# The B part of the scan's operand built per tile in the first stage, readout ahead of the inputs in two banks, and the weighing by C whole and one unit later

## The reference

```python
x = x + 0.5 * ffn(layernorm(x), w1, b1, w2, b2)
x = x + mamba(layernorm(x), ...)
x = x + 0.5 * ffn(layernorm(x), w1, b1, w2, b2)

# mamba, D_INNER 512, D_STATE 16
xc = silu(causal_conv(xn @ W_in.T))
dt = soft_clamp(softplus(xc @ W_dt.T + b_dt), 0.001, 0.1, 0.5)
Bp, Cp = xc @ W_B.T, xc @ W_C.T
dA = exp(soft_clamp(dt * A, -8, 8, 0.5))
def step(h, ...):
    h = h * dA_t + dt_t * B_t * x_t
    nrm = sqrt(sum(h * h))
    h = where(t % 10 == 0, h * minimum(20 / nrm, 1), h)
    y = sum_n(h * C_t) + D_param * x_t
out = x + scale * (y * silu(gate)) @ W_out.T
```

## Time and profile before

| | |
|---|---|
| median of 3 runs | 1645.36 us (1644.27 to 1646.35) |
| the profiled execution | 1644.98 us, its span 1643.1 us |
| busy, share of the span | PE 89%, DVE 78%, ACT 68%, POOL 60% |
| first stage, a tile | 49.7 us (226.03 to 275.73, the same instruction of two tiles) |
| scan stage, 410 units | 428.3 to 1426.4 us |

### The profile page before, as it was taken

How to read it: one execution, slowest core, us unless ns; L and a number is a source line. 1 busy time by engine, 2 the same in 40 slices (tenths; PEclk the granted TensorE clock), 3 DMA queues, 4 the chain that set the end, 5 groups by cost and what they waited for, 6 DMA issues and landing times. The chain is left out here.

```text
span 1643.1 us, 24197 instructions
## 1 busy us (share of the span) xinstructions
PE 1461.6 (89%) x6460; PEld 986.7 (60%) x6460; DVE 1278.2 (78%) x2555; ACT 1112.3 (68%) x2515; POOL 986.4 (60%) x1350
## 2 busy tenths in 40 slices
PE   6999999999688888888888888888888888999998
PEld 5555555554456566656665656665665665677776
DVE  7657656655578888888887888887888889877885
ACT  4355445557978888888887888887888874243333
POOL 1202222012479898989988889898998999700000
PEclk9999999999789999999999999999999999999999
DMA  7222355125565555656655565555655436465430
GB/s 251 77 79 91 117 146 143 66 92 189 164 182 158 162 152 140 172 149 168 160 154 151 137 174 133 158 161 141 178 153 155 135 98 198 122 208 171 137 116 26
DMA packets 232654, 236.84 MB, mean 144 GB/s; under 512 B 46120, under 2 KB 198376, under 8 KB 232520
## 3 DMA queue, kind: packets, MB, share of 16 engines
q1 hardware_dynamic: 231576, 233.99, 49.7%
q10 hardware_dynamic: 944, 1.31, 0.2%
HBM read 136.84 MB, written 98.68 MB: 143 GB/s over the span
## 5 line engine op out<-in xcount | busy, mean ns | idle before, releaser
L1145 DVE TENSOR_TENSOR_SCAN h<-decay,banks 128x352 f32<-128x352 f32 x820 | 710.5, 882 | 56.8 <-POOL hc L948 1.5
L948 POOL TENSOR_TENSOR hc<-h,bc 128x320 f32<-128x320 f32 x820 | 655.1, 821 | 30.6 <-PE banks L995 28.4
L995 PE MATMUL banks<-hc,w_ident 128*128 128x320 f32 (+1 forms) x1664 | 543.6, 452 | 47.6 <-ACT yc L1084 38.6
L1050 ACT ACTIVATE tb<-dtc,a 128x320 f32<-128x320 f32 (+1 forms) x832 | 416.3, 554 | 4.8 <-DVE x L562 4.8
L995 PEld LDWEIGHTS banks<-hc,w_ident 128*128 128x128 f32 x1664 | 291.8, 196 | 125.5 <-POOL hc L948 39.8
L1072 ACT ACTIVATE decay<-tb 128x640 f32<-128x640 f32 x410 | 296.3, 723 | 0.4
L938 POOL TENSOR_TENSOR rc<-qs,w_mhalf 128x1 f32<-128x1 f32 x410 | 225.9, 551 | 114.9 <-DVE qs L1129 106.0
L983 PE MATMUL banks<-ub 128*128 128x176 f32 x1640 | 283.9, 297 | 10.9 <-DMA ub<-scratch_ub 10.9
L976 PEld LDWEIGHTS banks<-sc_ss,sc_ones 128*128 128x128 f32 x820 | 134.6, 197 | 263.8 <-ACT sc_sq L1061 246.2
L1061 ACT ACTIVATE sc_sq<-h 128x64 f32<-128x64 f32 x410 | 128.1, 313 | 189.1 <-issue 100.0
L983 PEld LDWEIGHTS banks<-ub 128*128 128x128 f32 x1640 | 227.4, 201 | 12.2 <-DMA ub<-scratch_ub 11.2
(11 more groups left out here) (117 smaller groups left out, 1562.1 us busy)
## 6 DMA issues: line engine op xcount, KB each, us to landing
ub<-scratch_ub SPq DMA_DIRECT2D x410, 107.5 KB
bc<-scratch_blk SPq DMA_DIRECT2D x205, 160.0 KB, 3.6
scratch_ub<-turned SPq DMA_DIRECT2D x64, 512.0 KB, 4.1
scratch_ub<-spread SPq DMA_DIRECT2D x64, 176.0 KB, 4.3
scratch_xc<-xc SPq DMA_DIRECT2D x8, 1024.0 KB, 4.8
scratch_sg<-sg SPq DMA_DIRECT2D x8, 1024.0 KB, 5.9
scratch_dt<-dt SPq DMA_DIRECT2D x8, 1024.0 KB, 5.9
scratch_u<-u SPq DMA_DIRECT2D x8, 1024.0 KB, 6.7
```

Source lines behind the costliest of these rows:

```text
L948: pool.tensor_tensor(hc[:, pl % 2, x * kh * B * N:(x + 1) * kh * B * N, j % QB * S:(j % QB + 1) * S] .rearrange("p (c b n) e -> p c b n e" ...
L995: mm = pe.matmul(psY[:, 0:KE * B * wide], w.ident[:], rhs, start=(n == 0), stop=(n == N - 1))
L1050: act.activation(tanh_rows(c, r), dtc[:, c % 2, k * B:(k + 1) * B, 0:blocks_of(c) * S].rearrange("p b (k e) -> p k b e", e=S), ACT.Tanh, s ...
L1145: dve.tensor_tensor_scan(state(m).rearrange("p r e -> p (r e)")[:, half], decay[:, m % DRING, half], psI[m % B][:, half], 0.0, ALU.mult, A ...
```

## The change

- **Weighing**: `weigh(m)` is one operation over all of the state, where it was two halves, and POOL issues `weigh(m-1)` in its turn m.
- **Readout**: in PE's turn m the readout's two matmuls (now for m-1) stand between `total(m+2)` and `inputs(m+2)`; they stood behind `inputs(m+2)`. Quads alternate between two PSUM banks (2 and 5) up to quad 48, and wait for the copy of the quad before the last (`y_before`); `copy_y` comes two units later.
- **B**: it is no longer part of the pieces. PE turns it out of `bcs` for each tile (`turn_b`, a new slot `bt` in the ring), ACT copies it (`copy_bt`), POOL splits and spreads it (`spread_b`, six operations a tile into two buffers), SP stores it (`store_b`, 8 DMAs a tile). The masks are made at tile 0.
- **Pieces**: u alone, one each 10 units, PE's four transposes in four units, ACT's copy in two halves, DVE's part after that; loads and stores at other places of SP's order.
- **Stores**: `dt` and `u` of the last tile go out in eight parts, one a block.

```diff
@@ sync (first stage)
             if i in (6, 7):
                 scan.load_piece(sp, i - 5)
                 scan.store_piece(sp, i - 6)
+            if i >= 2:
+                scan.store_b(sp, i - 2, 0, G)
             sp.wait_ge(xc_ready, 2 * (i + 1))
...
                 scan.load_units(sp)
+                scan.store_b(sp, LAST - 1, 0, G)
@@ gpsimd (first stage)
                 norm2(i + 1)
-            if i in (6, 7):
-                scan.mask_piece(pool, i - 6)
+            if i >= 1:
+                scan.spread_b(pool, i - 1, 0, G)
@@ tensor (first stage)
             project(i, "x", 0)
+            if i >= 1:
+                turn_b(i - 1)
@@ scan stage
+    def spread_b(pool, i, q0, q1):
+        if q0 == 0:
+            pool.wait_ge(pre.ring_read, pre.turn_of["bt", i, 0] + 1)
+            if i >= 1:
+                pool.wait_ge(spread_done, G * i)
+            pool.tensor_copy(bts[:, 0], bt[:]).then_inc(b_split, 1)
+            pool.wait_ge(b_split, 2 * i + 1)
+            pool.tensor_tensor(bts[:, 1], bt[:], bts[:, 0].bitcast(F32), ALU.subtract).then_inc(b_split, 1)
...
+        for q in range(q0, q1):
+            if G * i + q >= 2:
+                pool.wait_ge(b_out[q % 2], 2 * 16 * ((G * i + q) // 2))
+            pool.tensor_tensor(
+                spread[:, q % 2], bts[:, :, q].bitcast(F32).unsqueeze(3).broadcast_to([P, 2, N, W]),
+                mask[:, (i * TT // P + q % 2) % (S // 2)].unsqueeze(1).unsqueeze(1).broadcast_to([P, 2, N, W]),
+                ALU.mult).then_inc(spread_done, 1)
+
+    def store_b(sp, i, q0, q1):
+        for q in range(q0, q1):
+            t = i * TT + q % 2 * P
+            sp.wait_ge(spread_done, G * i + q + 1)
+            for half in range(2):
+                sp.dma_start(
+                    dram["ub"][q // 2, t:t + P].rearrange("t (r h) x -> t r h x", h=2)[:, :, half, E:],
+                    spread[:, q % 2].bitcast(F32).rearrange("p r n e -> p r (n e)")).then_inc(b_out[q % 2], 16)
@@ gpsimd (scan stage)
-            weigh(m, 0)
-            weigh(m, 1)
-            if m - 1 in pieces:
-                mask_piece(pool, pieces[m - 1])
+            if m >= 1:
+                weigh(m - 1)
+            if m in (8, 12, 16, 20):
+                spread_b(pool, TILES - 1, m // 4 - 2, m // 4 - 1)
+        weigh(UNITS - 1)
@@ tensor (scan stage)
         for m in range(UNITS):
             if m + B < UNITS:
                 total(m + B)
-                inputs(m + B)
-            if m in pieces:
-                turn_piece(pe, pieces[m], psT)
...
-            p, part = m // (QB * B) - 1, m % (QB * B)
+            p, part = (m - 1) // (QB * B) - 1, (m - 1) % (QB * B)
             if p >= 0:
                 readout(p, part * each, (part + 1) * each)
+            if m + B < UNITS:
+                inputs(m + B)
+            for c in range(KE):
+                if m - c in pieces:
+                    turn_piece(pe, pieces[m - c], psT, c, c + 1)
```

More of the change, by code:

```diff
@@ L142, in store_dt_u, with store_last, stored @@
         store(sp, "u", u[:], u_out, i)
+    def store_last(sp, k):
+        name, tile, ready, done = ("dt", dt, dt_ready, dt_out) if k < KE else ("u", u, u_ready, u_out)
+        c = k % KE
+        sp.wait_ge(ready, LAST + 1)
+        sp.dma_start(dram[name][:, c * B:(c + 1) * B, steps(LAST)],
+                     tile[:, c, :].rearrange("p (b t) -> p b t", b=B)).then_inc(done, 16)
+    def stored(i):
+        return 16 * (i + 1) if i < LAST else 16 * (LAST + KE)
     def dt_u(dve, i):
@@ L347, in project_bc, with turn_b @@
             mm.then_inc(ring_done, 1)
+        def turn_b(i):
+            out = fill(("bt", i, 0))
+            pe.wait_ge(ring_read, use["bc", i, 0] + 1)
+            for q in range(G):
+                mm = pe.transpose(out[:, q * N:(q + 1) * N], bcs[0:N, q * P:(q + 1) * P], w.ident[0:N, 0:N])
+            mm.then_inc(ring_done, 1)
         pe.wait_ge(consts, 1)
@@ L838, in high_piece, with turn_piece @@
[L838 to L843, removed]
-    def low_piece(dve, k, src):
[L846 to L858, removed]
+    def turn_piece(pe, k, out, c0, c1):
+        if c0 == 0:
+            pe.wait_ge(piece_in, 16 * (k + 1))
+            if k >= 1:
+                pe.wait_ge(ut_lo, k)
+        for c in range(c0, c1):
+            mm = pe.transpose(out[:, c * P:(c + 1) * P], piece[:, c, :], w.ident[:])
+        if c1 == KE:
+            mm.then_inc(ut_done, 1)
@@ L861, in store_piece @@
         t, b = k // B * P, k % B
-        rows = dram["ub"][b, t:t + P].rearrange("t (r h) x -> t r h x", h=2)
         sp.wait_ge(ut_lo, k + 1)
         for r in range(2):
-            sp.dma_start(rows[:, r, :, 0:E], turned[:, :, 0:E].bitcast(F32)).then_inc(ub_out, 16)
-        sp.wait_ge(spread_done, k + 1)
-        for half in range(2):
-            sp.dma_start(rows[:, :, half, E:], spread[:].bitcast(F32).rearrange("p r n e -> p r (n e)")
-                         ).then_inc(ub_out, 16)
+            sp.dma_start(dram["ub"][b, t:t + P, 2 * r:2 * r + 2, 0:E], turned[:].bitcast(F32)).then_inc(ut_out, 16)
@@ L1117, in scalar @@
                 decays(m + AHEAD)
-            if m % (QB * B) == 0 and m >= 2 * QB * B:
+            if m % (QB * B) == 2 and m >= 2 * QB * B:
                 copy_y(m // (QB * B) - 2)
-            if m in pieces:
-                high_piece(act, pieces[m], psT)
-        for p in range((UNITS - 1) // (QB * B) - 1, QUADS):
+            for x in range(2):
+                if m - KE - x in pieces:
+                    high_piece(act, pieces[m - KE - x], psT, x * E // 2, (x + 1) * E // 2)
+        for p in range((UNITS - 3) // (QB * B) - 1, QUADS):
             copy_y(p)
```

154 lines of the change are left out of this document (95 added, 59 removed).

## The result

The changed kernel takes **1717.21 us** (median of 4 runs, 1715.12 to 1720.2) against 1645.86 us (4 runs, 1644.27 to 1647.84): a ratio of **1.0434**, 95% interval 1.0415 to 1.0454. It is slower by 71 us, and the forecast was 1716. The span grew by 70.2 us, to 1713.3.

What follows compares the result with a forecast made beforehand. PE bounds the first stage; in the scan no engine is free of load and stalls add 100 us. First stage +49 and scan +22 give +71 us, 1716 us; range 1664 to 1750, chance of slower 0.90.

Steps and rivals of the forecast that it cites:

- First stage: Tiles ahead of the scan: spreads waiting for stores delay `rstd1` and DVE, with clock loss and transposes; +49 us (33 to 65).
- R: The time in a first-stage tile at which POOL ends `norm2`; `rstd1` was forecast at R + 7.4 to R + 11.0.
- The clock term: PE in the first stage loses clock after each of four pauses, 1.5 us each: 6 us (0 to 10).
- the stalls: First-stage tiles 2 to 5: 3 x 6.5 + 20.3 = 40 us (33 to 47) from `rstd1` behind `spread_b`.
- `turn_b`, 3 us: Four added transposes a tile on busy PE in the first stage, seven times: 3 us, 8 at the high end.
- The loop: Scan: with the readout ahead of the inputs, a two-unit loop from squares to squares takes 4.87 us, 2.44 a unit.
- the rival's point of decision: Scan unit of 2.27 us, the readout adding 0.28 us in place of 0.60, decides whether the first rival holds.
- Scan: Unit of 2.44 against 2.40 us gives +15 us; with pieces, late loads and ends +22 us (0 to +45).
- left over: Scan: disturbances remaining beside the regular unit, pieces 3 us and late `ub` loads 5.2 us, taken as 8 us.
- up to the 100 us: Scan: stalls of 0.27 us per unit, 100 us in all, which the second bank and spread pieces take away.
- the first rival: Scan gains what was removed: units stay at 2.13 us, scan falls 92 us, time 1602; chance 0.08.
- these rivals: First stage doesn't stall: 1670, chance 0.10. PE falls to half clock in the scan: near 1990, chance 0.03.

Runs made afterwards that it cites:

- Kernel 1: The changed kernel with POOL issuing the next turn's `rstd1` ahead of `spread_b` in the first stage instead of behind it: 1675.7 us.
- kernel 5: The changed kernel with `rstd1` ahead of `spread_b` in the first stage and the inputs ahead of the readout in the scan: 1608.6 us.
- Kernel 7: The changed kernel with one of the readout's two matmuls ahead of the inputs and the other behind them: 1652.8 us.
- Kernel 2: The changed kernel with PE issuing the inputs ahead of the readout's two matmuls in the scan, as before the change: 1648.7 us.
- kernel 11: The changed kernel with inputs ahead of the readout and the weighing in two halves, still one unit later: 1651.2 us.
- kernel 3: The kernel before with only the readout and the pieces' transposes placed as in the changed kernel; one bank, halved weighing: 1822.8 us.
- 8: The changed kernel, readout ahead of the inputs, with one PSUM bank for all quads and the copy one unit earlier: 1829.4 us.
- 9: The changed kernel with inputs ahead of the readout and the weighing in two halves in its own unit again: 1802.9 us.

## Why the prediction held, point by point

- **First stage, +49 forecast, +47.0 measured.** The mechanism was read rightly: SP behind `bc` at R + 2.7, `rstd1` at R + 8.6 where the bounds were 7.4 and 11.0, DVE's waits 12.65 and 26.63 us ("some 11", "some 26"), PE's pauses ahead of the gate 5.1 to 10.1 us. The stores are issued in 0.62 us and land in 2.4 (medians up to 425 us), near the low ends: the queues were as empty as supposed. The tiles 2 to 5 are 7.34, 8.17, 21.73 and 7.71 us longer than 49.7, 45 in all. Kernel 1 shows the cause.
- **The clock term, 6 us.** PE was at 0.50 behind the pauses. The gate's 16 matmuls took 8.82, 8.97, 9.22 and 9.83 us in the four tiles, 8.3 us in all over the 7.13 of the earlier trace rows, against my 6. The Trainium skill (TensorE: Matmul & The Clock Gate, section on HAM oscillation) tells of a PE that comes back at half clock from each long wait for data; by it all four pauses pay, and the rows agree. Without these 8.3 the four tiles have some 37 us, where I had 40 for the stalls: two small errors that cancel.
- **`turn_b`, 3 us.** Its four transposes take 0.42 us a tile, and seven times that is 3; in the one tile of kernel 5 that takes 49.70 us again, PE's pause ahead of the gate is 0.08 us where it was 0.60, so there they cost nothing. The masks and copies at 0 weren't tried alone.
- **The loop.** 4.87 us forecast, 4.84 measured. Of its parts the readout holds the inputs up for 0.92 us (722.95 - 722.03), not 1.10, and from the inputs' start to the carry it is 0.93 us, not 0.79: again two errors that cancel. "Nearly evenly" was wrong: units alternate between 2.70 and 2.14 us. Kernel 7 shows that the cost sets in at a certain length, as the rival's point of decision had it.
- **Scan, +22 forecast, +23.9 measured.** From 485 to 1380 us there are 363 carries, 2.466 us a unit. The loop makes 2.42 of it, a little under the 2.435 forecast (6 us), and 0.046 a unit, 17 us, is left over, where I had 8. One term of it was too small for certain: a unit with a piece takes some 3.00 us and the one behind it 2.12, so that a piece adds 0.28 us to its loop and not 0.1.
- **What the forecast of the scan had wrong beside its sum.** It let the stalls of before go, "up to the 100 us", and the first rival built on that with "100 less 8 left over". Kernel 2 measures 49 us removed, and 73 added by the order. 409 units of 2.13 us are 871, and kernel 2 still has 78 us above that: pieces (30 times 0.88), quads' copies (some 48 times 0.53), the eight tail units (8 times 1.84), and the rest. Where the loop is 4.84 us long most of this lies within it: 409 units longer by 0.29 us would be 119 us, and only 73 show. That it would be hidden so is nowhere in the forecast, and in this the forecast was lucky. The first rival's 1602 us was too low by 47, as kernel 2 shows, even had its condition held.
- **What was removed.** The second bank gives 17 us and the spread of the pieces 13. That makes 30 of 49; what gives the rest (POOL's spread out of the scan, or the places in SP's order) wasn't tried.
- **Rivals.** The first stage does stall, and PE keeps 0.99 in the scan. Both went against these rivals as the trace of before said.

## What to carry to other kernels

Where an instruction may wait, ask what stands behind it on its engine: a wait for a copy of like size cost 17 us behind the inputs and 112 ahead of them (there with a lower clock), and `rstd1` behind a wait for a store cost 39. In a loop of several engines added work costs little as long as the loop is no longer than the work of the engine that sets the pace: half of the readout cost 11 us of the scan, all of it 73. And stalls and a longer loop don't simply add: where the loop is long, stalls lie within it, and where it is short again, they show; the kernel with both orders repaired is at 1608.6 us.

## What the runs showed that was not expected

**DVE beside POOL.** In eight of the last units of the scan DVE has an operation on 512 elements for the output; in four of them it multiplies by the gate. Timelines of kernel after, then of kernel 11 (halves):

```profile
1469.86 1.44 POOL L1031 TENSOR_TENSOR hc<-h,bc 128x640 f32<-128x640 f32 x1
1469.91 1.94 DVE L1510 TENSOR_TENSOR q_ys<-q_ys,q_sg 128x512 f32<-128x512 f32 x1
```
```profile
1404.84 2.03 POOL L1030 TENSOR_TENSOR hc<-h,bc 128x320 f32<-128x320 f32 x2
1404.88 1.31 DVE L1510 TENSOR_TENSOR q_ys<-q_ys,q_sg 128x512 f32<-128x512 f32 x1
```

The same operation takes 1.94 us beside a whole weighing, 1.31 beside halves (in the kernel before too), and 0.68 with no weighing beside it, at 1517.00 us of kernel after. It ends 0.55 us after POOL's call does (1469.86 + 1.44 = 1471.30, and 1471.85). With halves it ends 0.54 us after the first call's 0.81, and the second ends late: the two take 2.03 us in place of 1.60. The Trainium skill (SBUF — State Buffer, section on the two separate sides) says that DVE with two SBUF inputs and GpSimd share a pair of ports as an exclusive lock, and the loser waits for the whole instruction; the rows agree. So the whole call lengthens eight tail units from some 3.34 us, before and in kernel 11, to 3.96 or more in after, some 5 us that I had counted as 0. DVE's `xn` in 1 is slowed beside POOL too, from 1.38 to 2.44 us; it is another form, and why it is slowed wasn't tried.

**The clock.** In kernel 3 PE paused for about 1.6 us ahead of 551.67, with shorter pauses before it, and then worked at 1.2 GHz: its readout took 2.47 us in place of 1.32. Kernels 3, 8 and 9 show a granted clock of 0.94, 0.94 and 0.89 from 485 to 1380 us, against 0.99 in after. A long wait in each quad is thus paid twice, as a wait and as slower work behind it.
